# Scan stage: transposes in place of matmuls for the states, and the residual added by an accumulating transfer from a token-major x1

## The chip, the cores and the metric

One Trainium2 (trn2) chip, one of its cores. The metric is the time of one execution on the device in microseconds (us), the median of several runs. The engines are TensorE (PE; its weight loads are listed as PEld), VectorE (DVE), ScalarE (ACT), GpSimd (POOL) and SyncE (SP, which issues transfers). ACT and POOL issue transfers too; accumulating ones, which add to what stands at the destination, are issued by POOL.

## What is computed

The reference is a two-layer metaformer on x of shape (64, 56, 56, 128), float32, batch x height x width x channels; a token is one of the 3136 positions of an image. In short:

```
x = x + attention(ln_c(x))                     # windows of 7 x 7, shifted by 3, 4 heads
t = x as (64, 3136, 128)
wx = batchnorm(ln(t) @ W.T) * gamma + beta
y[0] = 0;  y[k+1] = sigmoid(wx[:, k] + y[k] @ V.T)     # a scan over the 3136 tokens, 64 images at once
t = t + y                                      # <- the residual that the change is about
x = t + conv(ln_c(t))                          # per token and channel: gates, 16 steps of a complex recurrence
out = x + experts(ln(x))                       # 64 experts, 8 tokens each
```

The kernel computes sigmoid(a) as 0.5 (1 + tanh(a / 2)); its state is the tanh, so that the sum with the residual is x1 + 0.5 * tanh + 0.5.

## The kernel before

Three stages follow each other. **Attention** (`attention_phase`, L83) goes image by image, 64 of them, about 79 us each. At an image's end SP stores x1 = x + attention (L205) and xh = its normalised form (L207) to DRAM, both laid out image by image: 3136 runs of 512 bytes, next to each other within an image. Then SP loads XL and XR of later images (L197, L201). POOL needs XR to add the bias of the projection (L257).

**Scan** (`scan_phase`, L624) has the recurrence over 3136 tokens. It works in chunks of TF = 128 tokens (25 chunks, the last of 64), and a chunk in NO = 4 slots of K = 32 steps (`slots`, L744). Step k of a slot is one PE matmul of the state with `vh` into PSUM (L1267) and one tanh on ACT (L1136) into XU, which holds states as [channel, token, image]. Each needs the one before it, so PE and ACT take turns, and whatever either does between two steps stands in its queue between them.

What is woven in is work on an earlier chunk, in groups of OS = 16 images (`oc` is the group, NGR = 100 of them, one a slot), one chunk behind the scan, and a slot later the heavier part of the same group (`o`):

- PE `turn_u(oc, q)` (L1225), four a group (q = 0 to 3), each on four images. A matmul of X2 (x1 as loaded) with the identity fills bank pY and four matmuls of the states with `hident` (half the identity) add the states, turned to [token, image, channel]. ACT `residual(oc, q)` (L1101) copies pY to X2 with the bias 0.5. For s = 0 they stand at k = 0 to 3 and 1 to 4, since the chunk must first be scanned to its end; for the groups of s = 1, 2, 3 they are done in the slot before, at k = 24, 26, 28, 30 and 25, 27, 29, 31. Slot s = 3 has no late ones.
- SP `load_x1(o)` (L778) loads X2 a group ahead, from image-major x1 in runs of 512 bytes, once the store three groups back has landed.
- DVE `statistics(oc)` (L931): mean and variance of X2, when all four residuals are done; at the head of DVE's part of the slot for s > 0, after L1023 for s = 0.
- POOL: three small operations give the scale (L848 to L852). ACT then normalises (L1152, k = 10 to 13), PE turns the result (`turn_normal`), and the gate matmuls follow, one a step, from k = 16 (L1296), each read by ACT (L1113, L1115). A slot ends on ACT with Exp and Ln over the group (L1194, L1196) and two loads of activation tables.
- DVE L1010 to L1072 does the 16 steps of the complex recurrence in closed form for group `o`, ACT helps with Squares (k = 6, 8, 14, 16, 20, 22).
- POOL adds by accumulating transfers, each within SBUF: Dl to BX (L861), the first half of the result to X2 (`add_state`, L817) and the second (`add_input`, L825), the latter at the head of the next slot, when the former has landed. SP then stores X2 (L794).
- `turn_inputs` (L1238) and `keep_turned` (L1088) bring the next chunk's xh in: ACT loads XQ (L1086), PE transposes, ACT copies to XU.

X2 has three buffers (NX = 3). **Experts** (`expert_phase`, L1299) come last.

The order on each engine is written out by hand: for each slot, for each k, in the order of the code. Nothing is planned by costs.

Of the kernel before, what the change touches and what calls it, by code (L numbers as in the profile page):

```python
# [21 lines left out]
P = 128  # L22
# [37 lines left out]
def tokens_of(dram, b):  # L60

    return dram[bass.ds(b, 1)].rearrange("a (n r) w c -> (a r w) n c", r=2)

# [19 lines left out]
def attention_phase(nc, B, x, w_qkvT, qkv_bias, w_projT, proj_bias, rel_table, mask, ident_d, ones_d,  # L83
# [3 lines left out]
    with ExitStack() as ctx:  # L87
# [94 lines left out]
        def _(sp):  # L182
# [10 lines left out]
            def body(m, prev, main, nxt):  # L193
# [8 lines left out]
                if prev:  # L202
                    q = m.step(-1)
                    wait(sp, x1_sb, m.idx * NG)
                    sp.dma_start(tokens_of(x1_d, q.idx), XR[q.par][:]).then_inc(x1_st[q.par], 16)  # L205
                    wait(sp, xh_sb, m.idx * NG)
                    sp.dma_start(tokens_of(xh_d, q.idx), XH[q.par][:, :, 0:C]).then_inc(xh_st[q.par], 16)  # L207
# [416 lines left out]
def scan_phase(nc, B, x1_d, xh_d, gram, w_ffnT, v_ffnT, gamma, beta, w_gates, b_gates, dft, kernA, kernB,  # L624
# [37 lines left out]
    with ExitStack() as ctx:  # L662
# [37 lines left out]
        hident = sb("hident", [P, P])  # L700
# [18 lines left out]
        x2_ld = [sem(f"x2_ld{i}") for i in range(NX)]  # L719
        x3_st = sem("x3_st"); first_added = sem("first_added"); both_added = sem("both_added")  # L720
# [40 lines left out]

        @block.sync
        def _(sp):
# [14 lines left out]
            def load_x1(o):  # L778
                c, s = divmod(o, NO)
                wait(sp, x3_st, (o - NX + 1) * 16)  # L780
                sp.dma_start(X2[o % NX][0:size(c)], tokens(x1_d, OS * s, OS, c)).then_inc(x2_ld[o % NX], 16)

            load_x1(0)
            for j, s, oc, o, scan, prep in slots():
                if oc is not None and oc + 1 < NGR:
                    load_x1(oc + 1)
# [4 lines left out]
                if o is not None:  # L791
                    c, s_ = divmod(o, NO)
                    sp.wait_ge(both_added, (o + 1) * 16)
                    sp.dma_start(tokens(x3_d, OS * s_, OS, c), X2[o % NX][0:size(c)]).then_inc(x3_st, 16)  # L794
            sp.wait_ge(x3_st, NGR * 16)

        @block.gpsimd
        def _(pool):
# [12 lines left out]
            pool.tensor_tensor(fld[4], fld[3], nhalf[:, 0:C], ALU.pow).then_inc(pch, 1)  # L811

# [16 lines left out]
            for j, s, oc, o, scan, prep in slots():  # L829
                if o is not None and o >= 1:  # L830
                    add_input(o - 1)
                if scan and s == NO - 2:
# [25 lines left out]
                if oc is not None:  # L858
# [3 lines left out]
                                   accum_op=ALU.add).then_inc(bx_d, 16)  # L862
                if o is not None:
                    add_state(o)
# [3 lines left out]
        def _(dve):  # L868
# [41 lines left out]
            dve.tensor_scalar(hident[:], ident[:], 0.5, None, ALU.mult)  # L910
# [20 lines left out]
            def statistics(oc, tc):  # L931
                dve.wait_ge(x2_d, oc * NQ + NQ)
# [144 lines left out]
        def _(act):  # L1077
# [4 lines left out]
            def load_xq(i):  # L1082

                j, b = divmod(i, NO * NQ)
                if j < NCH:
                    act.dma_start(XQ[i % 2][0:size(j)], tokens(xh_d, Q * b, Q, j)).then_inc(xq_ld[i % 2], 16)  # L1086
# [14 lines left out]
            def residual(oc, q):  # L1101

                tc = size(oc // NO)
                act.wait_ge(y_ps, oc * NQ + q + 1)
# [684 lines left out]
```

## Time and profile before

| | us |
|---|---|
| median of 3 runs (13234.78 to 13243.13) | 13239.91 |
| the profiled execution | 13252.06 |
| its span, first to last instruction | 13250.1 |

A profile shows one execution. A row of the timeline gives the start, the duration, the engine, the line of the kernel and the operation, what it writes and reads, and in brackets how long the engine sat idle before it and whose end released it.
### The profile page before, as it was taken

To read this page: it belongs to the slowest core of one execution; us is meant where nothing else is said; L and a number is where in the kernel's file an instruction comes from. 1 tells how busy PE (TensorE), PEld (TensorE's weight loads), DVE (VectorE), ACT (ScalarE), POOL (GpSimd) and SP (SyncE) were. 2 spreads that over 40 slices of the span, in tenths; PEclk is the share of its full clock that TensorE was granted. 3 is DMA by queue.
4 is the path that set the end of the run, shared out by engine and by line. 5 is a ranking of instruction groups with operands and counts; after the bars stand their busy time and mean duration, and the time that the engine had idled before them with its cause. 6 is when DMAs were issued, how large, how long until landed. Compare 5 with 4: busy or idle time off the path is not lost. (4 is left out here: it accounts for less than half of the span.)

```text
span 13250.1 us, 228029 instructions
## 1 busy us (share of the span) xinstructions
PE 10057.1 (76%) x79510; PEld 7477.3 (56%) x79510; DVE 10189.2 (77%) x22622; ACT 9128.6 (69%) x21751; POOL 5150.9 (39%) x4755
## 2 busy tenths in 40 slices
PE   7888888888888886777777777777777777355544
PEld 5666666666666665555555555555555555133343
DVE  6777777777777774488888888888888889899910
ACT  6888888888888885466666666666666666476710
POOL 4444445444444443112212212222122122188866
PEclk9999999999999998677777777777777777677755
DMA  3333333333333332244444444444444444476544
GB/s 71 79 80 84 88 86 80 80 79 81 84 89 83 79 80 79 53 103 100 108 99 107 104 99 109 99 104 105 100 110 99 103 101 95 66 137 122 99 80 69
DMA packets 1642383, 1215.93 MB, mean 92 GB/s; under 512 B 65493, under 2 KB 1542168, under 8 KB 1603620
## 3 DMA queue, kind: packets, MB, share of 16 engines
q1 hardware_dynamic: 1345060, 756.57, 24.0%
q0 software_dynamic: 89088, 341.98, 14.0%
q10 hardware_dynamic: 207104, 102.79, 2.8%
q8 instruction: 649, 10.63, 0.3%
q14 instruction: 482, 3.95, 0.1%
HBM read 567.56 MB, written 325.32 MB: 67 GB/s over the span
## 5 line engine op out<-in xcount | busy, mean ns | idle before, releaser
L1267 PEld LDWEIGHTS s_pW<-s_XU,s_vh 128*128 128x128 f32 x6272 | 1414.0, 253 | 1884.9 <-ACT s_XU L1136 1574.5
L1267 PE MATMUL s_pW<-s_XU,s_vh 128*128 128x64 f32 x6272 | 1464.6, 325 | 1020.4 <-ACT s_XU L1136 1020.4
L1136 ACT ACTIVATE s_XU<-s_pW 128x64 f32<-128x64 f32 x3136 | 717.9, 229 | 1947.2 <-PE s_pW L1267 1927.7
L1296 PE MATMUL s_pG<-s_wg,s_XNT 128*128 128x384 f32 (+1 forms) x3200 | 1507.8, 560 | 15.4 <-ACT s_Z L1115 15.4
L409 ACT ACTIVATE KB<-pV,qkb 32x392 f32<-32x392 f32 x2048 | 1188.2, 580 | 25.7 <-PE pV L499 1.9
L249 POOL TENSOR_TENSOR SS<-SS,mx 128x784 f32<-128x784 f32 x512 | 768.7, 1501 | 805.7 <-DVE mx L342 805.5
L817 POOL DMA_DIRECT2D s_X<-s_f x100 | 87.1, 871 | 2190.4 <-DVE s_f L1067 2120.0
L1234 PEld LDWEIGHTS s_pY<-s_hident,s_XU 128*128 128x128 f32 (+1 forms) x3200 | 750.8, 305 | 174.4 <-issue 126.2
L257 POOL TENSOR_TENSOR XR<-XR,pbias 112x512 f32<-112x512 f32 x448 | 570.6, 1274 | 648.2 <-DMA XR<-in_x_dram 648.2
L461 ACT ACTIVATE XH<-XR,nm,rs 112x128 f32<-112x128 f32 x1792 | 731.3, 482 | 90.5 <-POOL nm L268 82.0
L507 PE MATMUL pS<-KB,QT 128*64 128x196 f32 x8192 | 793.3, 336 | 0.0
L529 PE MATMUL pV<-wq,XT 128*49 128x64 f32 x16384 | 564.6, 222 | 249.3 <-ACT KB L409 248.9
L507 PEld LDWEIGHTS pS<-KB,QT 128*64 128x64 f32 x8192 | 545.0, 137 | 352.8 <-issue 286.0
L353 DVE RECIPROCAL rc<-pO 128x16 f32<-128x16 f32 x512 | 131.3, 256 | 793.3 <-PE pO L550 793.3
L1152 ACT ACTIVATE s_f<-s_X,s_nmr,s_rst 128x128 f32<-128x128 f32 (+1 forms) x1600 | 652.9, 485 | 121.8 <-POOL s_nmr L852 121.7
L550 PE MATMUL pO<-Vb,PT 128*64 128x66 f32 x16384 | 591.5, 225 | 168.4 <-DVE gram L347 164.6
L1234 PE MATMUL s_pY<-s_hident,s_XU 128*128 128x128 f32 (+1 forms) x3200 | 716.8, 369 | 0.0
L529 PEld LDWEIGHTS pV<-wq,XT 128*49 128x49 f32 x16384 | 489.1, 124 | 368.7 <-ACT KB L409 368.2
L861 POOL DMA_DIRECT2D s_BX<-s_Dl x100 | 90.6, 906 | 1519.5 <-DVE s_Dl L929 1488.9
L1222 PE MATMUL s_pW<-s_XU,s_ws 128*128 128x512 f32 x784 | 671.1, 953 | 1.2 <-ACT s_XU L1096 1.2
L550 PEld LDWEIGHTS pO<-Vb,PT 128*64 128x64 f32 x16384 | 522.2, 137 | 256.9 <-DVE gram L347 217.9
L1663 PE MATMUL e_pT<-e_ident,e_X 112*128 112x112 f32 x1792 | 307.4, 335 | 443.9 <-ACT e_X L1599 288.6
(263 smaller groups left out, 30132.9 us busy)
## 6 DMA issues: line engine op xcount, KB each, us to landing
XL<-in_x_dram SPq DMA_DIRECT2D x64, 1568.0 KB, 12.4
XR<-in_x_dram SPq DMA_DIRECT2D x64, 1568.0 KB, 18.0
x_dram<-XR SPq DMA_DIRECT2D x64, 1568.0 KB, 8.0
xh_dram<-XH SPq DMA_DIRECT2D x64, 1568.0 KB, 8.1
e_X<-out_dram SPq DMA_DIRECT2D x64, 1568.0 KB, 16.1
s_XQ<-xh_dram ACTq DMA_DIRECT2D x384, 256.0 KB, 3.3
s_BX<-s_Dl POOLq DMA_DIRECT2D x96, 1024.0 KB, 7.0
s_X<-s_f POOLq DMA_DIRECT2D x96, 1024.0 KB, 7.0
```

Of the source, the lines that this page charges most:

```text
L249: pool.tensor_tensor(sv[:], sv[:], mx[wi % 2][:].unsqueeze(2).broadcast_to([P, 16, L]), ALU.subtract).then_inc(s_sub, 1)
L409: i = act.activation(KB[par][r, :, h, :], pV[r, 0:NW * L].rearrange("c (w l) -> c w l", l=L), ACT.Identity, bias=qkb[r, 1:2])
L461: i = act.activation(XH[q.par][:, n0, 0:C], XR[q.par][:, n0, :], ACT.Identity, bias=nm2[:, k, t:t + 1], scale=rs2[:, k, t:t + 1])
L507: i = pe.matmul(pS[64 * s:64 * s + 64, p // 2, (p % 2) * NH * L:(p % 2 + 1) * NH * L], QT[par][:, w * L:w * L + 64], KB[par][:, w, :, :].r ...
L529: i = pe.matmul(pV[64 * o:64 * o + L, 64 * w:64 * w + 64], XT[im.par][:, wi, w, :], wq[:, 2 * C:3 * C].rearrange("c (a b d) -> c a b d", a ...
L550: i = pe.matmul(pO[64 * s:64 * s + 64, hp, 66 * p:66 * p + 66], PT[par][:, p, hp, 64 * s:64 * s + 64], Vb[par][:, w, hp, :], start=True, s ...
L1136: act.activation(XU[j % 2][:, t, :], pW[t // R % 2][:, B * (t % R):B * (t % R) + B], ACT.Tanh, scale=0.5).then_inc(u_sb, 1)
L1152: w = act.activation(XN[0:tc, i, :], X2[oc % NX][0:tc, i, :], ACT.Identity, bias=nmr[0:tc, i:i + 1], scale=rst[0:tc, i:i + 1])
L1222: pe.matmul(pW[r % 2][:, 0:R * B], ws[:], XU[j % 2][:, R * r:R * r + R, :].rearrange("c t b -> c (t b)"), start=True, stop=False, skip_gro ...
L1234: w = pe.matmul(pY[0:tc, C * i:C * i + C], XU[c % 2][:, 0:tc, OS * s + Q * q + i], hident[:], start=False, stop=True, skip_group_check=True)
L1267: pe.matmul(pW[t // R % 2][:, B * (t % R):B * (t % R) + B], vh[:], before, start=False, stop=True, skip_group_check=True).then_inc(z_ps, 1)
L1296: pe.matmul(pG[i % 3][0:tc, 0:3 * C], XNT[:, i, 0:tc], wg[:], start=True, stop=True).then_inc(g_ps, 1)
```

## The change

- x1 and xh are stored in DRAM with the token outermost, (3136, 64, 128): an image's store now writes 3136 runs of 512 bytes that lie 32 KB apart, and a group of the scan stage reads 16 images of a token as one run of 8 KB, XQ four images as one of 2 KB.
- `turn_u` no longer reads X2: its five matmuls become four transposes into pY, with the plain identity. `residual` scales by 0.5 as it copies.
- x1 is added to X2 afterwards by an accumulating transfer from DRAM, `add_x1`, issued by POOL when all four residuals of the group are done; DVE's statistics wait for it. `load_x1` on SP goes.
- The wait for the store of the buffer moves from SP's load to ACT's residual 0.
- The turns and residuals of the groups of s = 1, 2, 3 move seven steps forward, to k = 17, 19, 21, 23 and 18, 20, 22, 24.

The diff, cut where semaphores are declared:

```diff
+def token_rows(dram, b):
+    return dram[:, b, :].rearrange("(n t) c -> t n c", t=T)
...
-                    sp.dma_start(tokens_of(x1_d, q.idx), XR[q.par][:]).then_inc(x1_st[q.par], 16)
+                    sp.dma_start(token_rows(x1_d, q.idx), XR[q.par][:]).then_inc(x1_st[q.par], 16)
                     wait(sp, xh_sb, m.idx * NG)
-                    sp.dma_start(tokens_of(xh_d, q.idx), XH[q.par][:, :, 0:C]).then_inc(xh_st[q.par], 16)
+                    sp.dma_start(token_rows(xh_d, q.idx), XH[q.par][:, :, 0:C]).then_inc(xh_st[q.par], 16)
...
+        def rows_of(dram, b0, n, j):
+            return dram[j * TF:j * TF + size(j), b0:b0 + n, :].rearrange("t b c -> t (b c)")
...
-            def load_x1(o):
-                c, s = divmod(o, NO)
-                wait(sp, x3_st, (o - NX + 1) * 16)
-                sp.dma_start(X2[o % NX][0:size(c)], tokens(x1_d, OS * s, OS, c)).then_inc(x2_ld[o % NX], 16)
-
-            load_x1(0)
             for j, s, oc, o, scan, prep in slots():
-                if oc is not None and oc + 1 < NGR:
-                    load_x1(oc + 1)
...
+            def add_x1(o):
+                c, s_ = divmod(o, NO)
+                pool.wait_ge(x2_d, o * NQ + NQ)
+                pool.dma_start(X2[o % NX][0:size(c)].rearrange("t b c -> t (b c)"), rows_of(x1_d, OS * s_, OS, c),
+                               accum_op=ALU.add).then_inc(x1_added[o % 2], 16)
...
             for j, s, oc, o, scan, prep in slots():
                 if o is not None and o >= 1:
                     add_input(o - 1)
+                if oc is not None and s == 0:
+                    add_x1(oc)
...
                                    accum_op=ALU.add).then_inc(bx_d, 16)
+                if oc is not None and s + 1 < NO:
+                    add_x1(oc + 1)
                 if o is not None:
                     add_state(o)
...
-                dve.wait_ge(x2_d, oc * NQ + NQ)
+                dve.wait_ge(x1_added[oc % 2], (oc // 2 + 1) * 16)
...
-                    act.dma_start(XQ[i % 2][0:size(j)], tokens(xh_d, Q * b, Q, j)).then_inc(xq_ld[i % 2], 16)
+                    act.dma_start(XQ[i % 2][0:size(j)].rearrange("t b c -> t (b c)"), rows_of(xh_d, Q * b, Q, j)).then_inc(xq_ld[i % 2], 16)
...
+                if q == 0 and oc >= NX:
+                    act.wait_ge(x3_st[(oc - NX) % 2], ((oc - NX) // 2 + 1) * 16)
                 act.activation(X2[oc % NX][0:tc, Q * q:Q * q + Q, :].rearrange("t b c -> t (b c)"), pY[0:tc, :], ACT.Identity,
-                               bias=cols[0:tc, 1:2]).then_inc(x2_d, 1)
+                               bias=cols[0:tc, 1:2], scale=0.5).then_inc(x2_d, 1)
...
-                    if conv and s + 1 < NO and k in (25, 27, 29, 31):
-                        residual(oc + 1, (k - 25) // 2)
+                    if conv and s + 1 < NO and k in (18, 20, 22, 24):
+                        residual(oc + 1, (k - 18) // 2)
...
-                if q == 0:
-                    pe.wait_ge(x2_ld[oc % NX], (oc // NX + 1) * 16)
-                pe.matmul(pY[0:tc, :], ident[0:tc, 0:tc], X2[oc % NX][0:tc, Q * q:Q * q + Q, :].rearrange("t b c -> t (b c)"),
-                          start=True, stop=False, skip_group_check=True)
                 for i in range(Q):
-                    w = pe.matmul(pY[0:tc, C * i:C * i + C], XU[c % 2][:, 0:tc, OS * s + Q * q + i], hident[:],
-                                  start=False, stop=True, skip_group_check=True)
+                    w = pe.transpose(pY[0:tc, C * i:C * i + C], XU[c % 2][:, 0:tc, OS * s + Q * q + i], ident[:])
                 w.then_inc(y_ps, 1)
...
-                    if conv and s + 1 < NO and k in (24, 26, 28, 30):
-                        turn_u(oc + 1, (k - 24) // 2)
+                    if conv and s + 1 < NO and k in (17, 19, 21, 23):
+                        turn_u(oc + 1, (k - 17) // 2)
```

## Rows read from the trace of the kernel before

**Rows 1.** The page's first line.

```profile
span 13250.1 us, 228029 instructions
```

**Rows 2.** Windows: stretch and us, then PE, PEld, DVE, ACT, POOL busy, clock, DMA.

```profile
5281.00:11285.00 6004.00, 4558.12 (x17087) 3289.13 (x17086) 5005.98 (x5212) 3911.34 (x9961) 1318.57 (x722) 0.76 0.43 100
...
8128.16:8202.35 74.19, 53.95 (x206) 39.77 (x206) 60.61 (x78) 43.14 (x107) 13.39 (x10) 0.80 0.47 105
8202.35:8263.05 60.70, 45.88 (x178) 32.97 (x178) 51.29 (x55) 40.39 (x104) 9.14 (x11) 0.81 0.50 112
8263.05:8324.35 61.30, 46.94 (x176) 33.91 (x176) 55.53 (x63) 40.74 (x105) 25.70 (x9) 0.75 0.45 103
8324.35:8373.90 49.55, 39.23 (x146) 27.50 (x146) 43.34 (x26) 38.59 (x100) 5.20 (x4) 0.74 0.37 91
8017.35:8078.64 61.29, 46.96 (x176) 33.93 (x176) 55.52 (x63) 40.70 (x105) 25.68 (x9) 0.75 0.44 103
```

**Rows 3.** Timeline of PE around one slot's end and in the next.

```profile
8001.01 1.12 PE L1231 MATMUL s_pY<-s_X,s_ident 128*128 128x512 f32 x2
8001.97 1.81 PE L1234 MATMUL s_pY<-s_hident,s_XU 128*128 128x128 f32 x8
8003.62 0.81 PE L1296 MATMUL s_pG<-s_wg,s_XNT 128*128 128x384 f32 x2
...
8010.26 0.60 PE L1247 MATMUL s_pX<-s_ident,s_XQ 128*128 128x128 f32 x4
...
8021.24 1.06 PE L1247 MATMUL s_pX<-s_ident,s_XQ 128*128 128x128 f32 x4
...
8041.12 1.59 PE L1296 MATMUL s_pG<-s_wg,s_XNT 128*128 128x384 f32 x2
...
8057.02 1.08 PE L1222 MATMUL s_pW<-s_XU,s_ws 128*128 128x512 f32 x2
```

**Rows 4.** Timeline of ACT, steps 19 to 21 of a slot s = 2.

```profile
8047.44 0.22 ACT L1136 ACTIVATE s_XU<-s_pW 128x64 f32<-128x64 f32 x1 [2.01 <-PE s_pW L1267]
...
8048.31 0.22 ACT L1136 ACTIVATE s_XU<-s_pW 128x64 f32<-128x64 f32 x1 [0.21 <-PE s_pW L1267]
8048.43 1.14 ACT L1183 ACTIVATE s_f<-s_t,s_cols 128x1024 f32<-128x1024 f32 x1
...
8049.88 0.24 ACT L1136 ACTIVATE s_XU<-s_pW 128x64 f32<-128x64 f32 x1
```

**Rows 5.** Timeline of ACT in a slot s = 0: steps 2, 4 and 10.

```profile
8134.17 0.22 ACT L1136 ACTIVATE s_XU<-s_pW 128x64 f32<-128x64 f32 x1 [3.18 <-PE s_pW L1267]
...
8142.64 0.22 ACT L1136 ACTIVATE s_XU<-s_pW 128x64 f32<-128x64 f32 x1 [3.46 <-PE s_pW L1267]
...
8142.76 0.68 ACT L1105 ACTIVATE s_X<-s_pY,s_cols 128x512 f32<-128x512 f32 x1
...
8155.58 1.65 ACT L1152 ACTIVATE s_f<-s_X,s_nmr,s_rst 128x128 f32<-128x128 f32 x4 [3.91 <-POOL s_nmr L852]
```

**Rows 6.** Timeline of DVE in the same slot: the statistics.

```profile
8143.47 3.19 DVE L935 BATCH_NORM_STATS2 s_st<-s_X 128x6 f32<-128x128 f32 x16 [2.34 <-ACT s_X L1105]
```

**Rows 7.** Timeline of POOL in the same slot: the issue of `add_input`.

```profile
8135.69 0.86 POOL L825 DMA_DIRECT2D s_X<-s_Wv  x1 [7.35 <-DMA s_X<-s_f]
```

**Rows 8.** Transfers of the scan stage: size, median us from issue to landing.

```profile
s_X<-s_f POOLq DMA_DIRECT2D x96, 1024.0 KB, 7.0
s_X<-s_Wv POOLq DMA_DIRECT2D x96, 1024.0 KB, 6.9
out_dram<-s_X SPq DMA_DIRECT2D x96, 1024.0 KB, 5.6
...
s_X<-x_dram SPq DMA_DIRECT2D x93, 0.5 KB, 6.8
```

**Rows 9.** Attention: landing of L207, POOL's wait at L257, ACT in one image.

```profile
DMA to landing us min/median/max: 8.0/8.1/9.7
...
  DMA XR<-in_x_dram: 648.2, 64
...
2072.87 0.87 ACT L467 ACTIVATE PP<-SS 128x784 f32<-128x784 f32 x1 [1.03 <-POOL SS L249]
```

More of the change, by code:

```diff
@@ L699, in scan_phase @@
         ident = sb("ident", [P, P])
-        hident = sb("hident", [P, P])
         st = sb("st", [TF, OS, 6])
@@ L718, in scan_phase @@
         xq_ld = [sem(f"xq_ld{i}") for i in range(2)]
-        x2_ld = [sem(f"x2_ld{i}") for i in range(NX)]
-        x3_st = sem("x3_st"); first_added = sem("first_added"); both_added = sem("both_added")
+        x1_added = [sem(f"x1_added{i}") for i in range(2)]
+        x3_st = [sem(f"x3_st{i}") for i in range(2)]
+        first_added = sem("first_added"); both_added = sem("both_added")
         d_ld = sem("d_ld"); d_ps = sem("d_ps")
@@ L793, in _ @@
                     sp.wait_ge(both_added, (o + 1) * 16)
-                    sp.dma_start(tokens(x3_d, OS * s_, OS, c), X2[o % NX][0:size(c)]).then_inc(x3_st, 16)
-            sp.wait_ge(x3_st, NGR * 16)
+                    sp.dma_start(tokens(x3_d, OS * s_, OS, c), X2[o % NX][0:size(c)]).then_inc(x3_st[o % 2], 16)
+            for i in range(2):
+                sp.wait_ge(x3_st[i], NGR // 2 * 16)
         @block.gpsimd
@@ L908, in _ @@
             dve.scalar_tensor_tensor(ws[:], fld[0], 1.0 / C, ws[:], ALU.mult, ALU.add).then_inc(dch, 1)
-            dve.tensor_scalar(hident[:], ident[:], 0.5, None, ALU.mult)
             dve.memset(XU[1][:, TF - 1, :], -1.0).then_inc(ready, 1)
@@ L1711, in metaformer @@
         gram = ctx.enter_context(nc.sbuf_tensor("gram", [C, C + 1], F32))
+        x1_d, xh_d = (d.rearrange("b h w c -> (b h w) c").rearrange("(s b) c -> s b c", b=B) for d in (x1_d, xh_d))
         attention_phase(nc, B, A["x"], A["w_qkvT"], A["qkv_bias"], A["w_projT"], A["proj_bias"], A["rel_table"],
                         A["mask"], A["ident"], A["ones"], x1_d, xh_d, gram)
-        scan_phase(nc, B, x1_d.rearrange("b h w c -> b (h w) c"), xh_d.rearrange("b h w c -> b (h w) c"), gram,
+        scan_phase(nc, B, x1_d, xh_d, gram,
                    A["w_ffnT"], A["v_ffnT"], A["gamma"], A["beta"], A["w_gates"], A["b_gates"], A["dft"],
```

## The prediction, made before the changed kernel was built or run

> **What bounds the kernel now.** I read the views in this order. The page gives the span, 13250.1 us [rows 1]; its averages over three unlike stages say nothing of one of them. The windows show that the scan stage, 5281 to 11285 us, is 6004 us long, with VectorE (DVE) busy 83% of it, TensorE (PE) 76%, and, line by line, one chunk of four slots [rows 2]. A slot is the stretch between two table loads on ScalarE (ACT): 32 steps of the recurrence (k = 0 to 31), each a PE matmul and an ACT tanh, and woven into them the work on group `oc`. The four slots s = 0, 1, 2, 3 last 74.2, 60.7, 61.3 and 49.6 us, 245.7 us for the chunk, and full chunks repeat this. What sets them is the chain PE to ACT to PE: where PE has a `turn_u` between two steps, ACT sits idle 3.2 to 3.5 us before a tanh [rows 5]. DVE is busy 60.6 + 51.3 + 55.5 + 43.3 = 210.8 us of the 245.7 [rows 2], so 35 us a chunk are what any gain on the other engines can reach before DVE is the bound. Slot s = 3 shows the price of the work in question: it is the one without late `turn_u`, and 11.1 and 11.7 us shorter than s = 1 and s = 2.
>
> **The change, part by part.** *One turn on PE.* Now: a 512-column matmul pair (1.12 us, the next starts 0.96 later) and eight 128-column matmuls, until the gate matmul starts at 8003.62, 2.61 us after 8001.01 [rows 3]. After: four transposes. Four `turn_inputs` transposes take 0.60 us at 2.4 GHz and 1.06 at 1.2 GHz, of which the last 0.15 to 0.2 overlaps what follows [rows 3]: 0.45 or 0.9 us. The states are read with a stride of 256 bytes, those inputs are not; no row has a strided one-pass transpose. Bounds are 0.45 and half of what the eight strided matmuls take, 0.9; I take 0.45, since the transposes of the inputs are the same instruction but for the stride. Saved per turn: 2.15 us.
>
> *Late turns, slots 0 to 2.* They move from k = 24 to 30 to k = 17 to 23, the residuals from 25 to 31 to 18 to 24. At k = 17 and 19 PE is the later engine: +0.9 (low clock) and +0.45. At k = 18 the residual (0.68 us [rows 5]) hides behind PE. At k = 20 and 22 ACT is the later one, it has a Square of 1.14 us there and takes 1.57 us from tanh to tanh, against 0.87 where PE is the later one [rows 4]: +0.58 each, with the turns at 21 and 23 hidden behind it. At 24: +0.5. Sum 3.0 us in place of what s = 3 lacks; but some 0.9 of the 11.4 (the mean) are the `inputs` of k = 26 [rows 3], which slot 3 lacks too and which stay. 11.4 - 0.9 - 3.0 = 7.5, and 0.4 more since no residual stands ahead of the last gates: 7.9 us saved on the PE-ACT chain in each of three slots.
>
> *Early turns, slot 0.* Residual 3 ends at 8143.44, 15.3 us into the slot that begins at 8128.16; the steps there wait 3.2 and 3.5 us for PE [rows 5]. With turns of 0.9 us (I leave them at the low clock) the tanh of k = 2, 3, 4 come at 3.3, 6.3, 9.2 us instead of 6.0, 10.2 and 14.5, and residual 3 ends at 10.0: 5.3 us earlier. But the new transfer follows. `add_x1` is issued by POOL at 10.1, when the transfer of `add_input` (issued at 8135.69, 7.5 us into the slot, landing 6.9 us later at 14.4 [rows 7, 8]) is still under way. An accumulating transfer of 1 MB lands 7.0 us after its issue [rows 8]; from HBM none is seen, the nearest being the plain x1 load, 6.8 us. Bounds: 17.1 (side by side) and 21.4 (one after the other in full). I take 19.7, since issue and start-up of the second hide behind the first. Statistics so start 4.4 us later than now (8143.47, where DVE already waits 2.34 [rows 6]). Everything behind them moves by 4.4: POOL's three operations, then ACT's normalisation at k = 10, for which ACT already waits 3.91 us [rows 5], and whoever is queued behind it, the tanh of k = 11. So all of the 5.3 gained early is lost in that wait, and 4.4 more. Slot 0: 74.2 + 4.4 - 7.9 = 70.7 us.
>
> *Slots 1 to 3.* The PE-ACT chain alone would need 52.8, 53.4 and 49.6, together 155.8. DVE's own work in them is the chunk's 210.8 less a quarter for slot 0, and 0.4 more since slot 2 has `spectrum` and `bounded` besides: 158.5. DVE is now the later one: ACT waits for it at k = 6 (Square of t0). It keeps waiting about 1.6 us a slot for the Squares of k = 20 and 22, which the residual in front of each delays: +4.8. Slots 1 to 3: 163.3. Chunk: 70.7 + 163.3 = 234.0 against 245.7, so 11.7 saved.
>
> *Cover.* In slots 0 to 2 `add_x1(oc + 1)` waits on POOL for a residual that ends near step 24, some 14 us before DVE is through; `add_state`, queued behind it, is not due before that, and the 7 to 8 us of landing are over before the next statistics: nothing, as long as DVE is the bound; without that cover about 1 us a slot, since the seven steps of 0.87 that are left after k = 24 are that much shorter than the landing. ACT's new wait for the stored group holds back the tanh behind it; the store goes out once `add_input` has landed, 14.4 us into slot 0, and lands 5.6 later [rows 7, 8], at 20; the residual of k = 18 comes at 27 or later (k = 20 is at 8048.31 in the slot that began at 8017.35 [rows 2, 4]): nothing. SP loses a load and a wait, and nobody waits for its stores before that. Loads of XQ in runs of 2 KB for 512 bytes: no wait on them in this chunk, nothing. `hident` goes: nothing.
>
> *Attention.* x1 and xh are stored with the token outermost, each run of 512 bytes 32 KB from the last, on the queue on which the load of XR follows. Nearest row: the store as it is, 8.1 us to land [rows 9]. POOL waits for XR in each of 64 images, 648 us in all, and ACT then 1.03 us for POOL: so this load is on the path [rows 9], and every us by which the xh store is longer comes back some 63 times. Stores of x3 already jump (1.6 MB between runs) and land 1 MB in 5.6 us [rows 8], 187 GB/s against the 198 of the x1 and xh stores: I take 0, bounds 0 and one landing more (8.1 us, 510 in all).
>
> Sum: 23 full chunks with both halves x 11.7 = 269, the last ones taken at 0. The profiled execution took 13252 us (span 13250.1), so 12983; the median of the runs is 12 us below it: **12,971 us**, 2.0% faster. Its own range, 12,900 to 13,050: the landing's bounds (-2.6, +1.7 us a chunk), waits of DVE half or double (-2.4, +4.8), strided transposes (+1.3), all x 23 but not at once.
>
> **Rivals.** *Stores in attention get slower* (the other side). For: XR's load is on the path, and runs that are 32 KB apart have the same low address bits on all 16 engines. Against: the x3 store. It decides from 269 / 63 = 4.3 us more per store. With twice the landing: 13,480. With 2 us more, 13,095. The Trainium skill (DMA: Bandwidth & Descriptors, Latency and other measured facts) tells of rates that fall at row pitches of 2 MiB and more, not at 512 KiB; by that rule 32 KB would cost nothing; no row here has a pitch of a power of two, so nothing here bears it out or speaks against it.
>
> *The clock rises later.* PE runs the middle of a slot at 1.2 GHz (four transposes 1.06 us) and its end at 2.4 (0.60) [rows 3]; before the rise, some steps after 8041, it ran gate matmuls with hardly a gap. A gate matmul pair takes 1.59 us there and 0.81 after [rows 3]. If thinner PE work puts the rise off by two steps, 2 x 0.8 us x 3 slots x 23 = 110: 13,081. Against: s = 3 rises without any turn, its mean of 0.74 being close to s = 2's 0.75 [rows 2]. The Trainium skill (TensorE: Matmul & The Clock Gate, Part 4: PE-mode transpose) says that transposes do not count as activity; the trace cannot tell, since gates lie beside them. If it held, it would be this case.
>
> *DVE is not held back*: the add lands unqueued and the Squares are in time: up to 8 us a chunk more, 12,790. *It does not do what it says*, transposes as dear as the eight matmuls: PE saves only the 0.96 us of the 512-column pair a turn, some 3.7 us in each of slots 0 to 2, and slot 0 loses 4.4. Slots: 74.9, 57.0, 57.9 (DVE) and 52.3, 242.1 in all, 3.6 less than now: 13,157.
>
> **How the numbers follow.** Forecast 0.50; clock 0.13; stores 2 us slower 0.07; stores near the break-even (4.3 us, 13,240) 0.05; stores past it 0.17; DVE not held back 0.05; dear transposes 0.03. About 0.2% is what a measurement of this kernel can tell from no change. Faster 0.78 (forecast, clock, 2 us, DVE, dear transposes), same 0.05, slower 0.17. The range of 8 in 10 takes in the forecast, the clock, the slightly slower stores and the dear transposes: 12,870 to 13,190.
>
> **What would show it.** Right: chunks of 234 us; DVE over 88% busy in them; statistics in slot 0 waiting near 7 us for the add; ACT waiting at k = 6 in slots 1 to 3; POOL's wait for XR still 10 us an image and the attention stage 5281 us. Wrong: landing of the xh store over 10 us; gate matmuls of 1.6 us past k = 20; slots 1 to 3 ended by PE.

## The result, and the profile of the changed kernel

The changed kernel takes 13,168.1 us (median of 5 runs, 13,160.8 to 13,177.4) against 13,239.9 before: a ratio of 0.9946, 95% interval 0.9931 to 0.996. It is faster, by 72 us and not by the 269 that were forecast; 12,971 is 197 us off.

The page and the windows of the changed kernel, columns as in [rows 2]: the scan stage, then one chunk, slots s = 0 to 3.

```profile
span 13166.3 us, 223154 instructions
```

```profile
5302.20:11232.00 5929.80, 3883.46 (x14798) 2766.77 (x14796) 5023.53 (x5224) 3956.84 (x9975) 1502.01 (x821) 0.68 0.47 101
8334.48:8408.52 74.04, 41.66 (x165) 30.02 (x165) 53.97 (x53) 43.65 (x108) 12.95 (x9) 0.66 0.47 101
8408.52:8462.70 54.18, 40.74 (x154) 29.04 (x154) 51.48 (x52) 40.73 (x102) 9.69 (x7) 0.69 0.54 118
8462.70:8523.60 60.90, 40.46 (x152) 28.70 (x152) 52.95 (x56) 41.02 (x104) 31.23 (x13) 0.70 0.47 102
8523.60:8576.30 52.70, 37.16 (x140) 26.45 (x140) 52.05 (x60) 38.60 (x100) 8.16 (x5) 0.69 0.44 100
```

Beside [rows 2]: PE has lost part of its work (54, 46, 47 us busy in slots 0 to 2 became 42, 41, 40), DVE's is what it was over the chunk (210.8 us before, 210.5 now), and slot 1 is 6.5 us shorter. But slot 0, whose turns became cheaper too, is as long as before, and so is slot 2. POOL is busy 31.2 us in slot 2, 25.7 before. Each slot begins with the tanh behind ACT's table load; the mean of the 22 full chunks behind the first full one gives

| slots s = 0, 1, 2, 3 (us) | chunk | |
|---|---|---|
| 74.19, 60.75, 61.28, 49.52 | 245.7 | before |
| 70.7, and 163.3 for the three others | 234.0 | forecast |
| 73.42, 54.33, 60.75, 53.06 | 241.6 | after |

Slots 1 to 3 are 168.1 us, 4.8 over the forecast; slot 0 is 2.7 over. The whole difference of the spans, 84 us, adds up: the first full chunk 12.4, the 22 behind it 4.2 each (92), the last, short chunk -12, the attention stage -20.5 (first tanh of the scan at 5302.1, was 5281.6), what follows the scan 12. A minus marks a part that grew.

The waits of the scan stage (5600 to 11000 us) of the changed kernel: who waited for whom, us in all, times, the longest wait.

```profile
ACT s_XU L1149 <- PE s_pW L1275: 1031.0, 1422, 3.3
...
ACT s_f L1165 <- POOL s_nmr L862: 478.3, 47, 18.2
...
DVE s_st L946 <- DMA s_X<-x_dram: 204.5, 22, 10.1
ACT s_t L1170 <- DVE s_d L1026: 178.7, 67, 4.3
```

ACT's wait for PE, the one removed, was 1708.5 us. In its place stands the second line: ACT's normalisation at k = 10 waits for POOL in two slots of each chunk, 47 times, 478 us (before: 22 times, 87 us, all in slot 0). The forecast knew the wait in slot 0 alone.

**Slot 0.** Timelines of POOL, then of DVE, then of ACT in the slot that begins at 8334.48 (start, us, engine, line, operation, idle before it and who ended it).

```profile
8342.83 0.86 POOL L833 DMA_DIRECT2D s_X<-s_Wv  x1 [7.44 <-DMA s_X<-s_f]
8344.12 0.87 POOL L818 DMA_DIRECT2D s_X<-x_dram  x1 [0.43 <-ACT s_X L1118]
8361.35 2.19 POOL L858 TENSOR_TENSOR s_rst<-s_var,s_epst 128x16 f32<-128x16 f32 x1 [16.36 <-DVE s_var L85]
8363.62 4.87 POOL L860 TENSOR_TENSOR s_rst<-s_rst,s_nhalf 128x16 f32<-128x16 f32 x1
8368.56 0.67 POOL L862 TENSOR_TENSOR s_nmr<-s_mean,s_rst 128x16 f32<-128x16 f32 x1
```

```profile
8357.16 3.19 DVE L946 BATCH_NORM_STATS2 s_st<-s_X 128x6 f32<-128x128 f32 x16 [8.95 <-DMA s_X<-x_dram]
...
8361.18 2.28 DVE L939 TENSOR_TENSOR s_Wv<-s_IN,s_par_a 128x2048 f32<-128x2048 f32 x1
8363.39 2.30 DVE L940 TENSOR_TENSOR s_Dl<-s_IN,s_par_a 128x2048 f32<-128x2048 f32 x1
```

```profile
8369.26 1.65 ACT L1165 ACTIVATE s_f<-s_X,s_nmr,s_rst 128x128 f32<-128x128 f32 x4 [17.01 <-POOL s_nmr L862]
```

`add_x1` is issued 9.6 us into the slot (forecast 10.1), and its data are there at 22.7, 13.0 us later, where the median of all its transfers is 8.0. `add_input`, issued 1.3 us ahead of it, is still under way. Statistics, POOL's three operations (8 us for 16 values a row) and the normalisation follow in a row, as the forecast had it, from a start 3.0 us later than forecast.

**Slot 2.** Timeline of POOL, first of the changed kernel in the slot that begins at 8462.70.

```profile
8469.27 0.85 POOL L833 DMA_DIRECT2D s_X<-s_Wv  x1 [7.40 <-DMA s_X<-s_f]
8469.83 0.89 POOL L848 TENSOR_TENSOR s_par_b<-s_raw,s_twentieth 128x64 f32<-128x64 f32 x1
8470.79 1.25 POOL L849 TENSOR_SCALAR s_par_b<-s_raw 128x64 f32<-128x64 f32 x1
8472.10 1.10 POOL L850 TENSOR_SCALAR s_par_b<-s_raw 128x64 f32<-128x64 f32 x1
8473.27 2.18 POOL L851 TENSOR_SCALAR s_par_b<-s_raw 128x64 f32<-128x64 f32 x1
8475.52 2.10 POOL L858 TENSOR_TENSOR s_rst<-s_var,s_epst 128x16 f32<-128x16 f32 x1
8477.70 4.97 POOL L860 TENSOR_TENSOR s_rst<-s_rst,s_nhalf 128x16 f32<-128x16 f32 x1
8482.75 1.73 POOL L862 TENSOR_TENSOR s_nmr<-s_mean,s_rst 128x16 f32<-128x16 f32 x1
```

The same stretch of the kernel before, in the slot that begins at 8263.05, with its own line numbers.

```profile
8258.73 0.64 POOL L838 TENSOR_TENSOR s_par_b<-s_raw,s_twentieth 128x64 f32<-128x64 f32 x1
8259.43 0.38 POOL L839 TENSOR_SCALAR s_par_b<-s_raw 128x64 f32<-128x64 f32 x1
8259.87 0.37 POOL L840 TENSOR_SCALAR s_par_b<-s_raw 128x64 f32<-128x64 f32 x1
8260.30 0.37 POOL L841 TENSOR_SCALAR s_par_b<-s_raw 128x64 f32<-128x64 f32 x1
8261.45 1.15 POOL L848 TENSOR_TENSOR s_rst<-s_var,s_epst 128x16 f32<-128x16 f32 x1 [0.78 <-DVE s_var L80]
```

Before, `par_b` was begun 4.3 us ahead of the slot and took 2.0 us, and POOL then waited for the statistics. Now DVE, and with it the issue of `add_state` (8461.01), is through only as the slot in front ends; POOL stands until 8469.27 behind the landing of `add_state`, 6.6 us into the slot, and `par_b`'s 5.6 us come next, while the statistics are ready at 8468.2. `nmr` is finished at 8484.5, and there ACT starts:

```profile
8484.51 1.65 ACT L1165 ACTIVATE s_f<-s_X,s_nmr,s_rst 128x128 f32<-128x128 f32 x4 [4.98 <-POOL s_nmr L862]
```

### The profile page after: what moved, and what is told of

Same layout as the page of the kernel before. It is cut to its first block and busy times, and to the rows that moved or that the text cites. A ratio compares the mean times of both kernels' runs of the same rounds, so it can differ in the third digit from the quotient of the medians.

```text
span 13166.3 us, 223154 instructions
## 1 busy us (share of the span) xinstructions
PE 9361.3 (71%) x77110; PEld 6951.9 (53%) x77110; DVE 10186.9 (77%) x22621; ACT 9160.5 (70%) x21751; POOL 5335.9 (41%) x4855
## 5 line engine op out<-in xcount | busy, mean ns | idle before, releaser
L1275 PEld LDWEIGHTS s_pW<-s_XU,s_vh 128*128 128x128 f32 x6272 | 1462.3, 264 | 2039.3 <-ACT s_XU L1149 1755.8
L1275 PE MATMUL s_pW<-s_XU,s_vh 128*128 128x64 f32 x6272 | 1516.8, 335 | 1164.8 <-ACT s_XU L1149 1149.8
L262 POOL TENSOR_TENSOR XR<-XR,pbias 112x512 f32<-112x512 f32 x448 | 570.7, 1274 | 664.9 <-DMA XR<-in_x_dram 664.9
L1262 PE MATMUL s_pN<-s_ident,s_f 128*128 128x128 f32 (+1 forms) x800 | 210.8, 418 | 815.5 <-issue 426.6
L437 ACT COPY Vb<-pV 49x512 f32<-49x512 f32 x1024 | 597.6, 584 | 63.2 <-PE pV L534 4.7
L1304 PEld LDWEIGHTS s_pG<-s_wg,s_XNT 128*128 128x128 f32 (+1 forms) x3200 | 558.9, 212 | 140.9 <-issue 110.0
L1126 ACT ACTIVATE s_TG<-s_pG 128x256 f32<-128x256 f32 (+1 forms) x1600 | 618.6, 387 | 11.1 <-DVE s_Wv L1046 2.4
```

The costliest lines, as they stand in the source:

```text
L1126: act.activation(TG[0:tc, :, i, :], bank[:, 0:2 * C].rearrange("t (r c) -> t r c", r=4), ACT.Tanh, scale=0.5)
L1275: pe.matmul(pW[t // R % 2][:, B * (t % R):B * (t % R) + B], vh[:], before, start=False, stop=True, skip_group_check=True).then_inc(z_ps, 1)
L1304: pe.matmul(pG[i % 3][0:tc, 0:3 * C], XNT[:, i, 0:tc], wg[:], start=True, stop=True).then_inc(g_ps, 1)
```

## The experiments

Each experiment puts a theory against a rival, and what each of them expects stands ahead of its result. The theory: the forecast's mechanism is right, and two of its terms are off, both of them POOL's. One, in slot 0 the transfer of x1 is behind another one (2.7 us a chunk). Two, in slot 2 POOL's program order holds up `nmr` (the 4.8 us of slots 1 to 3). Its rivals: the transfer from HBM, or the new layout, is slow by itself; the place of the turns is what costs. Medians are of the timed runs, each ratio to the kernel before on the same chip with its 95% interval; slots are the means over full chunks.

| kernel | median us | ratio | first tanh | slots 0 to 3 | chunk |
|---|---|---|---|---|---|
| e1 layout only | 13,253.6 | 1.0011 (1.0002 to 1.002) | 5295.0 | 74.18, 60.75, 61.28, 49.53 | 245.7 |
| e2 image-major | 13,242.4 | 1.0004 (0.9995 to 1.0013) | 5292.9 | 77.34, 54.15, 60.73, 52.90 | 245.1 |
| e3 par_b late | 13,031.7 | 0.9847 (0.9834 to 0.986) | 5301.3 | 73.01, 54.09, 54.82, 53.81 | 235.7 |
| e4 add first | 12,953.9 | 0.9788 (0.9775 to 0.9801) | 5288.7 | 64.57, 54.18, 61.01, 52.80 | 232.6 |
| e5 both | 12,853.5 | 0.9709 (0.9696 to 0.9722) | 5298.6 | 65.44, 54.23, 54.86, 53.91 | 228.4 |
| e6 hold DVE | 13,062.0 | 0.9864 (0.9848 to 0.9879) | 5308.4 | 69.00, 54.12, 60.89, 52.90 | 236.9 |
| e7 old places | 13,204.7 | 0.9978 (0.9968 to 0.9987) | 5306.7 | 74.22, 55.20, 63.07, 51.26 | 243.8 |
| e8 moved only | 13,379.8 | 1.0109 (1.0093 to 1.0124) | 5288.4 | 72.24, 61.19, 65.50, 51.74 | 250.7 |
| e9 split | 12,780.7 | 0.9654 (0.9641 to 0.9667) | 5299.1 | 62.49, 54.08, 54.85, 53.75 | 225.2 |
| e10 before, par_b late | 13,237.4 | 0.9998 (0.9989 to 1.0007) | 5290.7 | 74.19, 60.75, 61.29, 49.52 | 245.7 |
| e11 before, hold DVE | 13,166.8 | 0.9946 (0.9933 to 0.996) | 5287.0 | 70.38, 61.05, 61.35, 49.55 | 242.3 |

### The layout: e1 and e2

e1 is the kernel before with `token_rows` and `rows_of` for its stores and loads, the turns unchanged. e2 is the kernel after with them undone:

```
-  sp.dma_start(token_rows(x1_d, q.idx), XR[q.par][:])        # xh likewise
+  sp.dma_start(tokens_of(x1_d, q.idx), XR[q.par][:])
-  pool.dma_start(X2[o % NX][0:size(c)].rearrange("t b c -> t (b c)"), rows_of(x1_d, OS * s_, OS, c), accum_op=ALU.add)
+  pool.dma_start(X2[o % NX][0:size(c)], tokens(x1_d, OS * s_, OS, c), accum_op=ALU.add)
```

> The kernel before with the new layout alone: x1 and xh are stored with the token outermost, and SP's load of x1 and ACT's of xh in the scan stage read one run per token; the turns and the matmuls stay as they were. The kernel after began its scan stage 20.6 us later than before (first tanh 5302.2 against 5281.6). Theory A (the token-major stores, one on the path of each image, cost 0.3 us an image): first tanh near 5302, the scan stage as before (6003 us), 13,260 us in all. Rival (the 20 us are no property of the layout, the stores cost nothing): first tanh near 5282 and 13,240 us. If the layout also brings transfers of XQ or x1 that land sooner and matter, the scan stage would be shorter than 6003; I expect within 10 us of it.

> The kernel after with the layout of before (image outermost): the accumulating transfer of x1 and the load of XQ gather runs of 512 bytes. Theory A (the stores cost 20 us in attention): first tanh near 5282, scan stage as in the kernel after (5910), 13,148 us. Rival (stores cost nothing; what the token-major layout buys is the transfer): first tanh unchanged at 5302, and the accumulating transfer of x1 in short runs lands 1 us or more later than the 8.0 of the kernel after, slot 0 longer by as much: 13,190 us or more.

e1 leaves the scan stage as it was, to a tenth of a microsecond a chunk, and costs 0.11%, some 15 us (3 to 26 by the interval): theory A, if less than its 20. Both stores still land in 8.1 us in the median; before, the one of x1 took 8.0 and that of xh 8.1 [rows 9]. Over all kernels here the first tanh comes at 5288 in the mean of the five image-major ones (5282 to 5293) and at 5300 in that of the eight token-major ones (5289 to 5308): about 12 us are the layout's, and the 20.5 of the first comparison are partly scatter. The 12 us stand in POOL's wait for the load of XR, which follows the stores on SP's queue (us in all, times; e1, then e2):

```profile
  DMA XR<-in_x_dram: 666.4, 64
```

```profile
  DMA XR<-in_x_dram: 652.6, 64
```

The two groups do not overlap: 648.2 to 654.0 us in the five image-major kernels, 658.1 to 666.4 in the eight token-major ones, 11 us apart in the mean. Why that load lands later behind stores that take no longer is open.

e2 shows what the layout buys. Transfers of x1 by accumulation, over the scan stage: median us from issue to landing, first the changed kernel, then e2.

```profile
s_X<-x_dram POOLq DMA_DIRECT2D x89, 1024.0 KB, 8.0
```

```profile
s_X<-x_dram POOLq DMA_DIRECT2D x89, 1024.0 KB, 10.2
```

In runs of 512 bytes the transfer takes 2.2 us more in the median. Slots 1 to 3 hide that and are as long as in the kernel after. In slot 0 the transfer stands behind another one and is on the path, and the slot is 3.9 us longer: 77.3 against 73.4. So e2 is at 13,242, where "13,190 or more" was expected for the case that the layout buys the transfer: without it the change gives nothing at all.

### POOL's order in slot 2: e3 and e10

```
     if oc is not None:
         ...                       # rst, three operations, up to nmr
     if scan and s == NO - 2:
+        ...                       # the four operations on par_b, which stood in front of rst
         pool.wait_ge(pr_d, j * 3 + 3)
```

> The kernel after, with POOL's four operations on par_b in slot 2 (5.6 us, they take the raw spectrum) moved behind the three operations on rst. Theory A (slot 2 is 3.0 us longer than forecast since ACT's normalisation at k = 10 waits for POOL, which does par_b first; ACT's step there is 7.8 us against 2.6 before): ACT's wait at k = 10 of slot 2 goes from about 5.2 us to near 0, since rst then ends 5.6 us earlier; slot 2 goes from 60.75 to about 57, 3 us or a little more a chunk, 70 to 85 us in all: 13,090. Rival (DVE is the bound of slot 2 anyway, as the forecast had it, and the wait at k = 10 only takes the place of one behind it): the wait goes and another on DVE at k = 20 or later grows by as much; slot 2 stays within 1 us: 13,150 to 13,168.

> The kernel before with POOL's four operations on par_b behind the three on rst, as in the kernel after, where it gave 136 us. Theory A (in the kernel before the order cost nothing, since ACT did not wait at k = 10 of slot 2, its step there being 2.57 us; the change uncovered it): slot 2 stays 61.3, 13,240, at most 20 less. Rival (POOL's order cost as much before the change, and the forecast missed a standing loss, not a new one): 13,100 to 13,150.

e3 takes 5.9 us from slot 2 (60.75 to 54.82) and 136 us from the whole, more than expected: the wait at k = 10 goes in full, and only 0.75 us of it come back in slot 3. POOL in slot 2 of e3, which begins at 7917.26:

```profile
7924.41 0.76 POOL L847 TENSOR_TENSOR s_rst<-s_var,s_epst 128x16 f32<-128x16 f32 x1
7925.24 3.80 POOL L849 TENSOR_TENSOR s_rst<-s_rst,s_nhalf 128x16 f32<-128x16 f32 x1
7929.12 0.56 POOL L851 TENSOR_TENSOR s_nmr<-s_mean,s_rst 128x16 f32<-128x16 f32 x1
```

`nmr` is ready 12.4 us into the slot instead of 21.8, and ACT's step at k = 10 takes 2.57 us as in the kernel before. Slots 1 to 3 are then 162.7 us. The forecast's 163.3, DVE's work and its small waits, is what these slots come to once POOL is out of the way. e10 has the same edit in the kernel before, and nothing moves (slot 2 61.29 for 61.28): the order cost nothing there. The change uncovered it.

### The transfers in slot 0: e4

```
+    if oc is not None and s == 0:
+        add_x1(oc)
     if o is not None and o >= 1:
         add_input(o - 1)
-    if oc is not None and s == 0:
-        add_x1(oc)
```

> The kernel after, with the accumulating transfer of x1 of slot 0 issued ahead of that of the gate's input instead of behind it. In the kernel after it lands 13 us after its issue, 22.7 us into the slot. Theory A (two accumulating transfers of 1 MB run one after the other, 7 us each): x1 lands 7.5 to 8 us after its issue, 17.5 us into the slot, the statistics start 5 us earlier and so does ACT's normalisation at k = 10; slot 0 goes from 73.4 to 69 or 70, 13,070 us (60 to 120 less than the kernel after). The input's transfer then lands at about 24, for which DVE waits 1 to 2 us in front of the products into Wv, not on that path. Rival (a transfer that accumulates into SBUF from HBM takes 13 us by itself): its landing stays at 13 us, statistics start at 22.5 as now, 13,168 us.

POOL, then DVE in slot 0 of e4, which begins at 7987.29:

```profile
7996.92 0.87 POOL L818 DMA_DIRECT2D s_X<-x_dram  x1 [8.75 <-ACT s_X L1118]
7997.46 1.22 POOL L833 DMA_DIRECT2D s_X<-s_Wv  x1
8009.30 0.21 POOL L858 TENSOR_TENSOR s_rst<-s_var,s_epst 128x16 f32<-128x16 f32 x1 [10.62 <-DVE s_var L85]
8009.59 2.93 POOL L860 TENSOR_TENSOR s_rst<-s_rst,s_nhalf 128x16 f32<-128x16 f32 x1
8012.60 0.61 POOL L862 TENSOR_TENSOR s_nmr<-s_mean,s_rst 128x16 f32<-128x16 f32 x1
```

```profile
8005.12 3.19 DVE L946 BATCH_NORM_STATS2 s_st<-s_X 128x6 f32<-128x128 f32 x16 [4.14 <-DMA s_X<-x_dram]
...
8010.84 2.29 DVE L939 TENSOR_TENSOR s_Wv<-s_IN,s_par_a 128x2048 f32<-128x2048 f32 x1 [1.63 <-DMA s_X<-s_Wv]
```

The transfer of x1 lands in 8.2 us when it goes first, and the other one, now behind it, at 8010.8, 13.3 us after its own issue. The second is there 5 to 6 us after the first, whichever leads, and the rival (the transfer is slow by itself) is out. Statistics come 4.9 us earlier, as expected. But slot 0 loses 8.9 us and the whole 214, where 60 to 120 were expected. The other 4 us stand in POOL's rows: its three operations span 3.9 us here and 7.9 in the kernel after. Here DVE had to wait for `add_input` and stood still until 8010.84, when POOL's second operation was under way; there it ran products of two SBUF operands from 8361.18 on.

### POOL beside a running DVE: e6 and e11

```
     wait(dve, both_added, o * 16)
+    if conv and s == 0:
+        dve.wait_ge(rs_d, oc + 1)
     turned_by(tm, Wv, inp, a, wp_d)
```

> The kernel after, with one wait more: in slot 0 DVE starts its products into Wv only when POOL has finished nmr. It tests why the kernel with x1's transfer first gained 8.9 us in slot 0 and not the 4.9 by which its statistics came earlier: there POOL's three operations behind the statistics took 4.0 us (0.21, 2.93, 0.61 each) while DVE stood still, in the kernel after 8.1 us (2.19, 4.87, 0.67) while DVE ran products of two SBUF operands. Theory A (DVE's running products slow POOL's small operations): with DVE held, the three take about 4.0 us again, ACT's normalisation at k = 10 comes 4 us earlier, slot 0 goes from 73.4 to 69.5, and 13,168 - 23 x 3.9 = 13,080; DVE starts its products 4 us later, which takes the place of the 5.1 us for which it waits for ACT two operations later. Rival (the 4.0 us came from transfers that were no longer under way, or something else of that kernel): the three still take 8 us, ACT's normalisation comes no earlier, 13,168; or, if DVE's delay counts, up to 13,240.

> The kernel before with DVE's products into Wv of slot 0 held until POOL has finished nmr, as in the kernel after, where it gave 106 us. In the kernel before ACT waits 3.91 us for POOL at k = 10 of slot 0. Theory A (POOL's three operations take 8 us beside DVE's products and 4 us without them, in this kernel too): ACT's wait goes, its step at k = 10 falls from 6.7 us to about 2.8, and slot 0 from 74.2 to 70.3: 13,240 - 23 x 3.9 = 13,150. Rival (here the transfers of the kernel after had to do with it, or DVE's delay of 4 us costs what POOL's gains): 13,240 or more.

POOL in slot 0 of e6 (it begins at 7812.68), then DVE:

```profile
7839.41 0.21 POOL L858 TENSOR_TENSOR s_rst<-s_var,s_epst 128x16 f32<-128x16 f32 x1 [16.33 <-DVE s_var L85]
7839.70 2.93 POOL L860 TENSOR_TENSOR s_rst<-s_rst,s_nhalf 128x16 f32<-128x16 f32 x1
7842.71 0.22 POOL L862 TENSOR_TENSOR s_nmr<-s_mean,s_rst 128x16 f32<-128x16 f32 x1
```

```profile
7843.06 2.29 DVE L939 TENSOR_TENSOR s_Wv<-s_IN,s_par_a 128x2048 f32<-128x2048 f32 x1 [3.74 <-POOL s_nmr L862]
```

One wait more on DVE makes the kernel after 106 us faster: slot 0 goes from 73.4 to 69.0, POOL's chain from 7.9 to 3.5 us, and DVE's late start takes the place of a wait it had anyway (5.1 us for ACT, two products later). e11 does the same to the kernel before, where the chain spanned 7.9 us too and ACT waited 3.91 us for it [rows 5]: slot 0 70.38 for 74.19, ratio 0.9946, as much as the whole change brought. So the slowing is a standing cost of slot 0 in both kernels. The Trainium skill (SBUF — State Buffer, section on SBUF's two separate sides) says that a DVE operation with two SBUF inputs and any GpSimd operation that reads SBUF exclude each other for a whole instruction. The trace agrees for a POOL operation that starts beside a running product: L858 took 2.19 us instead of 0.21 and ended at 8363.54, when DVE's L939 (8361.18, 2.28 us) had ended at 8363.46. In e4 L862 took 0.61 us instead of 0.22 and ended at 8013.21, when L939 had ended at 8013.13. The other way round it does not agree: in e4 L939 starts at 8010.84 inside L860, and takes its 2.29 us, and L860 its 2.93, as in e6, where each ran alone. So by these rows only POOL's operation is held up, and only when the product was there first; the spans of POOL's operations are rough in a profile.

### Both edits, and the transfer in two halves: e5 and e9

e9 has e5's edits, and `add_x1` for s = 0 in two halves of 8 images, the first behind residual 1 (DVE's wait counts both):

```
-    pool.wait_ge(x2_d, o * NQ + NQ)
+    h = 1 if s_ else 2
+    n = OS // h
+    for i in range(h):
+        pool.wait_ge(x2_d, o * NQ + NQ // h * (i + 1))
         ...                       # images n * i to n * i + n of X2 and x1
```

> Both edits of the two kernels that gained (12,954 with the transfer of x1 first, 13,032 with par_b late) in one. Theory A (they are two separate waits, one in slot 0, one in slot 2): slot 0 64.6, slot 1 54.1, slot 2 near 55, slot 3 near 54, together 227.5 a chunk, and 12,954 - 23 x 5.1 = 12,835. Rival (DVE is the bound behind both, and what one edit gives the other takes): 12,920 or more.

> The kernel with both edits (x1's transfer first in slot 0, par_b late; 12,853), and in slot 0 the transfer of x1 cut into two of 512 KB, the first issued after residual 1, the second after residual 3. Theory A (slot 0 is set by residual 3, then 1 MB of transfer, then the statistics and POOL's chain): the first half is under way from 6.5 us into the slot and the second lands 4 to 5 us after residual 3 instead of 8.2; statistics start 14 us into the slot instead of 17.8, slot 0 goes from 65.4 to 61.5 or 62, and 12,853 - 23 x 3.5 = 12,770. Rival (a transfer's cost here is its start and POOL's own issuing, not its bytes, or two of them cost more than one): statistics at 17 us or later, 12,840 to 12,900.

e5 is at 12,853, 36 us short of the sum of the two gains (136 and 214): slot 0 is 65.4, not 64.6, its steps at k = 2 and 3 being 1 us longer (why is open), and slot 3 is 53.9, not 52.8. By far the most of both gains is there, so the two causes are separate waits. Slots 1 to 3 are 163.0 us. POOL, then DVE, in slot 0 of e9 (it begins at 7694.88):

```profile
7699.46 0.87 POOL L821 DMA_DIRECT2D s_X<-x_dram  x1 [4.35 <-ACT s_X L1121]
7706.36 0.87 POOL L821 DMA_DIRECT2D s_X<-x_dram  x1 [6.03 <-ACT s_X L1121]
```

```profile
7711.82 3.19 DVE L949 BATCH_NORM_STATS2 s_st<-s_X 128x6 f32<-128x128 f32 x16 [3.91 <-DMA s_X<-x_dram]
```

The second half is there 5.4 us after its issue, statistics start 16.9 us into the slot, not at 14: the issue itself came at 11.5 because of the longer steps, and 512 KB cost 5.4 us and not 4 to 5. Still 73 us less, 12,780.7, the fastest kernel of this study, 3.5% under the kernel before.

### The place of the late turns: e7 and e8

e7 is the kernel after with turns at k = 24, 26, 28, 30 and residuals at 25 to 31; e8 is the kernel before with turns at 17, 19, 21, 23 and residuals at 18 to 24.

```
-  if conv and s + 1 < NO and k in (17, 19, 21, 23):
-      turn_u(oc + 1, (k - 17) // 2)
+  if conv and s + 1 < NO and k in (24, 26, 28, 30):
+      turn_u(oc + 1, (k - 24) // 2)
```

> The kernel after with its late turns back at k = 24, 26, 28, 30 and the residuals at 25 to 31. Theory A (the move of the turns is what lets the accumulating transfer of x1 be over before the next statistics; issued at the end of a slot it lands 8 us later): in slots 1 to 3 DVE waits for x1 at the start of the slot, up to 7 us, POOL's operations and ACT's normalisation follow later, and slots 1 to 3 grow by 3 to 6 us each: 13,168 + 23 x 13 = 13,470. By the forecast's own words the loss of that cover would be 1 us a slot: 13,240. Rival (the transfer is hidden either way and the move is worth only the steps): slots 0 to 2 grow by 1 to 2 us each, 13,250, and DVE does not wait for x1.

> The kernel before with its late turns at k = 17, 19, 21, 23 and residuals at 18 to 24, nothing else changed: turns by matmuls, x1 by SP's load. Theory A (the place is worth something by itself, since ACT has Squares at k = 20 and 22 that hide two of the turns in part, and no residual stands in front of the last gates): 1 to 2 us less in each of slots 0 to 2, 13,240 - 23 x 4 = 13,150. Rival (a turn by matmuls costs more there, at TensorE's lower clock, and holds up the Squares for which DVE waits): no gain or a loss, 13,240 to 13,330.

Both missed. Moving is worth 37 us in the kernel after, not 300: slots 0 and 1 grow by 0.8 and 0.9 us, slot 2 by 2.3, slot 3 shrinks by 1.8. The 2.3 us of slot 2 stand at k = 10, where ACT waits for `nmr` behind `par_b` (10.1 us for the step, 7.8 in the kernel after). DVE's wait for x1 is there, but it is short:

```profile
7950.54 3.19 DVE L946 BATCH_NORM_STATS2 s_st<-s_X 128x6 f32<-128x128 f32 x16 [3.56 <-DMA s_X<-x_dram]
```

That is DVE in a slot s = 1 of e7. What gives most of these 3.6 us back was not tried apart; ACT's steps at k = 20 and 22 are 1.57 us there and not 2.16, as its Squares do not stand behind a residual. The forecast's 1 us a slot without the cover was nearer than my expectation.

With turns by matmuls (e8) the same move costs 143 us, where a gain of 90 was expected. Slots 0 to 3 change by -2.0, +0.4, +4.2 and +2.2 us. A turn takes 3.5 us at k = 17, at the lower clock, and 2.6 at 19 to 23, all in front of the Squares, and DVE's wait for the Square of k = 20 grows from 186.7 us in 88 times to 425.0 in 65. But most of the loss stands at the place of POOL's order again: the step at k = 10 of slot 2 takes 6.9 us and not 2.6, behind `par_b`, though neither the turns nor x1's transfer had changed.

```profile
ACT s_f L1152 <- POOL s_nmr L852: 169.5, 44, 5.0
```

Before, that was 86.9 us in 22 times, all in slot 0. So e8 does not show that the move pays only with cheap turns: 4.3 of its 5.0 us a chunk stand at this step. That is read from the trace; the move with turns by matmuls and `par_b` late was not run.

## Why the prediction was right in kind and wrong in size

The measured 13,168 us is outside the forecast's own range of 12,900 to 13,050. It lies inside the range of 8 in 10, 12,870 to 13,190, whose upper part belonged to rivals that did not come about (slower stores, dear transposes at 13,157): that is luck. Two steps failed: in slot 0 the landing of `add_x1`, taken at 19.7 us into the slot, was at 22.7; in slots 1 to 3 POOL's chain, taken at nothing, cost 4.8 us a chunk.

**One turn on PE: right, near the upper bound.** PE of the changed kernel in a slot s = 1, the turn at k = 23 and the gate behind it:

```profile
8445.73 0.86 PE L1243 MATMUL s_pY<-s_ident,s_XU 128*128 128x128 f32 x4
...
8446.42 0.81 PE L1304 MATMUL s_pG<-s_wg,s_XNT 128*128 128x384 f32 x2
```

The next gate starts 0.69 us after the turn does, where 0.45 was taken and 0.9 was the bound, and 2.61 was the price before [rows 3]. The contiguous transposes of the inputs still take 0.60 us [rows 3], these 0.86. The stride is what differs between the two in the program; no run tries it alone.

**Late turns: right.** From tanh to tanh, the changed kernel takes, in medians over all slots s = 1, 2.46 us at k = 17 (1.71 before), 1.43 at 19 (0.87), 2.16 at 20 and 22 (1.57), 1.10 at 24 and 7.81 at 31 (3.37 and 8.24). The additions were forecast as +0.9, +0.45, +0.58 twice and +0.5 (at 24, on a plain step of 0.87), 3.0 in all, and came to 2.7; the gain at the end was forecast as 0.4.

**Early turns, slot 0: the landing's term was mis-sized.** Up to the issue of `add_x1` all is as forecast (9.6 us for 10.1). Then "I take 19.7, since issue and start-up of the second hide behind the first": it is 22.7, beyond the upper bound of 21.4. The bound was 6.9 + 7.0 us from the issue of `add_input` at 7.5; that issue came at 8.35, and the pair took 14.3 us. With 3.0 us on 70.7 the slot would be 73.7, and it is 73.4. What the step had right is that everything behind the statistics moves with them. What it left standing are POOL's 8 us beside DVE, a cost of the kernel before that e6 and e11 halve.

**Slots 1 to 3: right for DVE, and POOL was left out.** The step says "DVE is now the later one: ACT waits for it at k = 6". It does, 67 times. But it took POOL's chain for free, and the paragraph on the cover looked at `add_x1` and `add_state` only. Not seen was what stands between `add_input` and `nmr` in program order: a wait for a landing that DVE's pace sets, and `par_b`. In the kernel before POOL was through with `par_b` at 8260.7, 0.8 us before the statistics were ready, and the row for that was there to be read. 163.3 us were forecast, 168.1 came; with POOL's order mended 162.7 (e3) and 163.0 (e5). In the chunk of e3 that was read DVE is busy 157.6 us of them and idle 5.1, where 158.5 and 4.8 were forecast, so that sum was no luck. DVE is busy 210.5 us of the chunk's 241.8, 87% (forecast: over 88).

**Attention.** Forecast 0, with bounds up to 510 us. The stores' landings are unchanged and POOL's wait for XR went from 648.2 to 664.9 us in 64 images; some 12 to 15 us are lost (e1). The rival of slower stores is false. The rule of the Trainium skill that the prediction named (DMA: Bandwidth & Descriptors, Latency and other measured facts: row pitches of 2 MiB and more) would have 32 KB cost nothing, and the landings of the stores agree, 8.0 and 8.1 us before and after.

**The other rivals.** The clock does not rise later: the gate matmuls of slot 1 go from 1.48 to 0.81 us between the turns of k = 17 and 19, and none of 1.6 us comes past k = 20. The mean granted clock of the slots still fell, from between 0.74 and 0.81 [rows 2] to between 0.66 and 0.70. Its price shows at k = 5, a step of 1.05 us where it was 0.79 (medians, all four slots); the waits at k = 6 or 10 behind it take that in. "DVE is not held back" and "dear transposes" are false by the steps above. The sum of the misses: slot 0 2.7 x 22 = 59, slots 1 to 3 4.8 x 22 = 106, attention 21, the last chunk 12, less 12 behind the scan, together some 186, where 269 and the spans' 84 are 185 apart. The last chunk, of 16 steps a slot, was forecast at 0 and went from 207 to 219 us; it is 217 in e3, 212 in e4 and 209 in e5, so POOL's order and the order of the transfers made it there too.

## What to carry to other kernels

When one chain gets shorter, list for each queue what it does in program order between the event that moves and the next thing others wait for, the small operations too. That they cost nothing before does not say what they cost now. A new transfer on a queue is priced with the transfer ahead of it: here two of 1 MB took 14 us together, and the one that others wait for should go first. And if a short chain on POOL is on the path, look at what DVE does beside it: holding DVE back for some 4 us made both kernels faster.

## What the hardware showed that was not expected

POOL's three operations on 16 values a row span 3.5 us beside an idle DVE (0.21, 2.93, 0.22) and 7.9 us beside a DVE that runs products of two SBUF operands (2.19, 4.87, 0.67). Its four operations on 64 values take 2.0 us in the gap of the kernel before, 5.6 us in the kernel after and 9.4 us in e3, where they stand beside longer operations of DVE.

Two accumulating transfers of 1 MB, issued 0.5 to 1.3 us apart, land 8.2 and 13.3 us (e4) or 8.5 and 13.0 us (after) after their own issues: the one behind pays. When the second source was read in runs of 512 bytes in place of 8 KB, the transfer took 10.2 us instead of 8.0 in the median; half a transfer took 5.4 and 5.9 in the slot shown of e9.
